# A two-layer transformer on one Trainium2 core: moved work in the pipeline of the first cross attention

## The reference

```python
q = rmsnorm((latent @ wq.T).reshape(B, S_q, H, D), q_norm_w)        # latent = layernorm(x)
k = rmsnorm((inputs @ wk.T).reshape(B, S_kv, HK, D), k_norm_w)      # inputs = ctx
v = (inputs @ wv.T).reshape(B, S_kv, HK, D)
attn = softmax(einsum('bkgqd,bksd->bkgqs', q, k))
x = x + einsum('bkgqs,bksd->bkgqd', attn, v).reshape(...) @ wo.T
```

## Time and profile before

| what | value |
|---|---|
| median of 3 runs | 1685.0 us (1678.43, 1685.0, 1685.45) |
| the profiled execution's own time | 1682.17 us |
| its span, first to last instruction | 1680.3 us |
| busy in the span | PE 1481.5, PEld 1233.8, DVE 1252.9, ACT 1119.4, POOL 894.1 us |
| mean granted TensorE clock | 0.967 of full speed |
| the first attention | from the start to about 465 us |

### The profile page before, as it was taken

One profiled execution on the slowest core, in us unless ns is written; L12 is line 12 of the kernel. 1 busy time (PEld: TensorE's weight loads), 2 busy tenths in 40 slices (PEclk: granted clock), 3 DMA queues, 4 the chain that ended last, 5 costly groups with the idle time before them and its releaser, 6 DMA issues.

```text
span 1680.3 us, 38581 instructions
## 1 busy us (share of the span) xinstructions
PE 1481.5 (88%) x12380; PEld 1233.8 (73%) x12443; DVE 1252.9 (75%) x3064; ACT 1119.4 (67%) x2631; POOL 894.1 (53%) x789
## 2 busy tenths in 40 slices
PE   4898888888877989898886899999889899999888
PEld 3777777677766876676765688888767688888766
DVE  6888888888856557777774788888655677777656
ACT  4887777677744547766674577787633687778632
POOL 4667777677631114444430777777500777777500
PEclk9999999999999999989997899999999899999999
DMA  9700000000012221100000000000000000000000
GB/s 384 296 1 10 11 10 10 7 17 12 12 59 67 85 84 43 33 13 16 16 14 4 10 16 16 15 14 15 10 12 3 6 15 15 16 15 14 10 18 38
DMA packets 75554, 61.30 MB, mean 36 GB/s; under 512 B 40256, under 2 KB 61120, under 8 KB 74688
## 3 DMA queue, kind: packets, MB, share of 16 engines
q1 hardware_dynamic: 71360, 51.69, 9.5%
q0 software_dynamic: 4096, 8.40, 1.7%
HBM read 21.30 MB, written 30.41 MB: 31 GB/s over the span
## 4 chain that ended last, share of the span: by engine, by line
PE 63%; DVE 17%; issue 7%; ACT 7%; POOL 3%; DMA 1%; SPq 0%; DVEq 0%; POOLq 0%; ACTq 0%
PE slot L459 6%; PE slot L1631 6%; PE slot L461 5%; PE slot L460 5%; PE slot L1614 4%; PE slot L1575 4%; PE slot L1584 3%; PE slot L1310 3%; PE slot L1649 3%; PE slot L516 3%; PE slot L1865 3%; PE slot L1361 2%; ACT c_pT L1386 2%; PE slot L1625 2%; PE slot L1176 2%
## 5 line engine op out<-in xcount | busy, mean ns | idle before, releaser
L1032 POOL TENSOR_TENSOR rs<-mv,nhalf 128x1 f32 (+1 forms) x160 | 98.6, 616 | 292.3 <-DVE mv L1027 222.7
L1781 POOL TENSOR_TENSOR d_A<-d_A,d_B 128x1024 f32<-128x1024 f32 x64 | 150.7, 2354 | 133.5 <-DVE d_B L1727 133.4
L1785 POOL TENSOR_TENSOR d_r<-d_vv,nhalf 128x16 f32<-128x16 f32 x64 | 186.5, 2914 | 47.8 <-DVE d_vv L1749 47.5
L731 ACT ACTIVATE d_p<-slot,d_nm,d_r 128x128 f32<-128x128 f32 x512 | 185.9, 469 | 25.8 <-DVE d_nm L1740 25.8
L731 ACT ACTIVATE a_p<-slot,a_nm,a_rq 128x77 f32<-128x77 f32 x512 | 164.0, 429 | 36.1 <-DVE a_nm L755 36.1
L1631 PE MATMUL slot<-d_v,d_pT 128*128 128x65 f32 x1024 | 121.8, 272 | 1.4 <-ACT d_pT L1668 1.4
L731 ACT ACTIVATE c_p<-slot,c_nm 128x77 f32<-128x77 f32 x512 | 117.5, 361 | 7.3 <-DVE c_nm L1416 7.2
L1631 PEld LDWEIGHTS slot<-d_v,d_pT 128*128 128x128 f32 x1024 | 119.4, 192 | 2.1 <-ACT d_pT L1668 1.8
L1708 DVE TENSOR_TENSOR d_A<-slot,T 128x1024 f32<-128x1024 f32 x64 | 78.3, 1224 | 49.8 <-PE slot L1575 49.6
L1386 ACT ACTIVATE c_pT<-slot 77x1024 f32<-77x1024 f32 x64 | 65.7, 1027 | 73.5 <-PE slot L1310 73.4
L1736 DVE TENSOR_REDUCE slot<-slot 128x8 f32<-128x1024 f32 x64 | 78.9, 1232 | 31.3 <-PE slot L1614 28.5
(11 more groups left out here) (285 smaller groups left out, 4607.2 us busy)
## 6 DMA issues: line engine op xcount, KB each, us to landing
routed<-zero SPq DMA_DIRECT2D x2, 9216.0 KB, 48.9
b_x<-routed SPq DMA_DIRECT2D x80, 64.0 KB
answers<-b_y SPq DMA_DIRECT2D x40, 128.0 KB
X<-in_x SPq DMA_DIRECT2D x2, 1024.0 KB, 7.4
d_zx<-Z SPq DMA_DIRECT2D x64, 32.0 KB
H<-Z SPq DMA_DIRECT2D x64, 32.0 KB
out<-f_o SPq DMA_DIRECT2D x8, 256.0 KB, 2.0
d_zx<-Z SPq DMA_DIRECT2D x64, 31.8 KB
```

Of the source, the lines that this page charges most:

```text
L731: i = e.activation(t["p"][:, h, :], R[slot][:, k // nbank, nk * (k % nbank):nk * (k % nbank) + nk], ACT.Exp, bias=t["nm"][:, h:h + 1], sca ...
L1032: return e.tensor_tensor(rs[:, bass.ds(b, 1)], mv[:, bass.ds(b, 1), 1:2].rearrange("p a b -> p (a b)"), nhalf[:, 0:1], ALU.pow)
L1781: e.tensor_tensor(t["A"][:, p, :], t["A"][:, p, :], t["B"][:, p, :], ALU.add).then_inc(S("d_key"), 1)
L1785: e.tensor_tensor(t["r"][:, it.m(2, 4), :], t["vv"][:, p, :], nhalf[:, 0:16], ALU.pow).then_inc(S("d_key"), 1)
```

## The change

Six things move in the loop of the first attention; the arithmetic stays the same.

- TensorE: the projection of k and v comes directly behind that of q, ahead of the transposes of P. The router's transpose comes behind both halves of the scores instead of between them, and its logits between the two halves of P times v.
- The square of k is taken by ScalarE out of PSUM (a new ACTIVATE) instead of by GpSimd, ahead of the copies of k and v.
- VectorE: the sums of k's squares and the router's layer norm come ahead of the copy of the transposed P; the second `largest` comes ahead of the router's choice; the sum of q's squares and a_vvq come behind `added`. The largest values are written into a free corner of the scores' own PSUM tile instead of into a_mx in SBUF.
- GpSimd: rk and kn come first in the step, then the context and the scatters; it divides both halves of P, takes the root for the layer norm behind them and rq last.
- Start: VectorE takes the first statistics ahead of the mask, and GpSimd writes its constant tables ahead of the first roots; later groups of roots come behind kn in the steps 1 to 3.
- Semaphore counts follow (a_ev has four events a step instead of three, a_k two instead of three).

```diff
-                b = it.b(3)
-                if b is not None:
-                    for half in range(2):
-                        turned(it, half)
-                b = it.b(1)
-                if b is not None:
                     if it.seen(2):
                         e.wait_ge(S("a_qTe"), it.upto(2))
                     e.wait_ge(S("ac_cl"), count(b))
                     passes(e, R[1][0:SK, 0, :], [c[:, it.m(1, 4), :] for c in a["c"]], [w[:] for w in wkv0])\
                         .then_inc(S("a_pj"), 1)
+                b = it.b(3)
+                if b is not None:
+                    for half in range(2):
+                        turned(it, half)
...
-                        if half == 1:
-                            router(it)
...
-                else:
-                    router(it)
-                logits(it)
-                values(it)
+                router(it)
+                values(it, lambda: logits(it))
...
+                b = it.b(1)
+                if b is not None:
+                    e.wait_ge(S("a_pj"), count(b, 2, 3))
+                    if past(b - 1):
+                        e.wait_ge(S("a_var"), count(b - 1, 1, 4))
+                    e.activation(a["sqk"][0:SK, :], R[1][0:SK, 0, 0:256], ACT.Square).then_inc(S("a_ev"), 1)
...
-                e.tensor_reduce(a["mx"][:, h], s, AX.X, ALU.max, negate=True).then_inc(S(("ac_mxa", "ac_mxb")[half]), 1)
+                mx = R[slot][:, 0, 4 * SK:4 * SK + 8]
+                e.tensor_reduce(mx, s, AX.X, ALU.max, negate=True).then_inc(S(("ac_mxa", "ac_mxb")[half]), 1)
 
                 e.wait_ge(S("a_rq"), count(b))
                 e.wait_ge(S(("ac_mxa", "ac_mxb")[half]), count(b))
-                e.tensor_tensor(a["nm"][:, h], a["mx"][:, h], a["rq"][:, it.m(2, 2), h], ALU.mult)\
+                e.tensor_tensor(a["nm"][:, h], mx, a["rq"][:, it.m(2, 2), h], ALU.mult)\
...
-                second_half(it)
-                row_normed(it)
-                b = it.b(2)
-                if b is not None:
-                    largest(b, it, 0, 2)
-                row_turned(it)
...
-                    e.wait_ge(S("a_k"), count(b, 1, 3))
+                    e.wait_ge(S("a_ev"), count(b, 2, 4))
...
-                    e.wait_ge(S("a_ev"), count(b, 1, 3))
-                    e.tensor_reduce(a["ssq"][:], a["sq"][:].rearrange("p (h d) -> p h d", d=DH0), AX.X, ALU.add)\
-                        .then_inc(S("a_var"), 1)
+                row_normed(it)
+                second_half(it)
+                b = it.b(2)
+                if b is not None:
+                    largest(b, it, 0, 2)
+                row_turned(it)
+                b = it.b(2)
+                if b is not None:
+                    largest(b, it, 1, 3)
                 row_chosen(it)
                 group_placed(it)
                 group_chosen(it)
-                b = it.b(2)
-                if b is not None:
-                    largest(b, it, 1, 3)
-                b = it.b(1)
-                if b is not None:
-                    e.wait_ge(S("a_var"), count(b, 3, 4))
-                    if past(b - 1):
-                        e.wait_ge(S("a_rq"), count(b - 1))
-                    e.tensor_scalar(a["vvq"][:], a["ssq"][:], 1.0 / DH0, RMS_EPS, ALU.mult, ALU.add)\
-                        .then_inc(S("a_var"), 1)
                 b = it.b(2)
                 if b is not None:
                     sums(b, 0)
...
                 added(it)
+                b = it.b(1)
+                if b is not None:
+                    e.wait_ge(S("a_ev"), count(b, 1, 4))
+                    e.tensor_reduce(a["ssq"][:], a["sq"][:].rearrange("p (h d) -> p h d", d=DH0), AX.X, ALU.add)\
+                        .then_inc(S("a_var"), 1)
+                b = it.b(1)
+                if b is not None:
+                    e.wait_ge(S("a_var"), count(b, 3, 4))
+                    if past(b - 1):
+                        e.wait_ge(S("a_rq"), count(b - 1))
+                    e.tensor_scalar(a["vvq"][:], a["ssq"][:], 1.0 / DH0, RMS_EPS, ALU.mult, ALU.add)\
+                        .then_inc(S("a_var"), 1)
                 b = it.b(2)
                 if b is not None:
                     sums(b, 1)
-                    e.wait_ge(S("a_sum"), count(b, 4, 4))
-                    normalize(e, a, slice(8, 16), SK).then_inc(S("ac_nb"), 1)
                 measured(it)
...
@@ -1055,42 +1058,42 @@
             def body(it):
                 if it.static and it.i == 7:
                     e.wait_ge(S("cleared0"), 16)
-                b = it.b(0)
-                if b is not None:
-                    split_context(e, a, it, b)
                 b = it.b(1)
-                if b is not None:
-                    e.wait_ge(S("a_ev"), count(b, 2, 3))
-                    if past(b - 1):
-                        e.wait_ge(S("a_var"), count(b - 1, 1, 4))
-                    e.tensor_tensor(a["sqk"][0:SK, :], a["kr"][0:SK, :], a["kr"][0:SK, :], ALU.mult).then_inc(S("a_k"), 1)
-                scatter(e, it)
                 if b is not None:
                     e.wait_ge(S("a_var"), count(b, 2, 4))
                     e.tensor_tensor(a["rk"][0:SK, :], a["vvk"][0:SK, :], nhalf[0:SK, 0:4], ALU.pow).then_inc(S("a_k"), 1)
-                    e.wait_ge(S("a_k"), count(b, 2, 3))
+                    e.wait_ge(S("a_ev"), count(b, 3, 4))
+                    e.wait_ge(S("a_k"), count(b, 1, 2))
                     if past(b - 1):
                         e.wait_ge(S("a_pj"), count(b - 1, 3, 3))
                     e.tensor_tensor(a["kn"][0:SK, :, :, :],
                                     a["kr"][0:SK, :].rearrange("p (h d) -> p h d", d=DH0).unsqueeze(2).to_broadcast([SK, 4, 2, DH0]),
                                     a["rk"][0:SK, :].unsqueeze(2).unsqueeze(3).to_broadcast([SK, 4, 2, DH0]),
                                     ALU.mult).then_inc(S("a_k"), 1)
+                if it.static and 1 <= it.i < NB // ST:
+                    first_roots(e, it.i)
+                b = it.b(0)
+                if b is not None:
+                    split_context(e, a, it, b)
+                scatter(e, it)
                 b = it.b(2)
                 if b is not None:
                     e.wait_ge(S("a_sum"), count(b, 2, 4))
                     normalize(e, a, slice(0, 8), SK).then_inc(S("ac_na"), 1)
+                b = it.b(2)
+                if b is not None:
+                    e.wait_ge(S("a_sum"), count(b, 4, 4))
+                    normalize(e, a, slice(8, 16), SK).then_inc(S("ac_nb"), 1)
+                b = it.b(4)
+                if b is not None:
+                    e.wait_ge(S("ac_ve"), count(b))
+                    root(e, b).then_inc(S("ac_rs"), 1)
                 b = it.b(1)
                 if b is not None:
                     e.wait_ge(S("a_var"), count(b, 4, 4))
                     if past(b - 2):
                         e.wait_ge(S("ac_expb"), count(b - 2))
                     e.tensor_tensor(a["rq"][:, it.m(1, 2), :], a["vvq"][:], nhalf[:, 0:16], ALU.pow).then_inc(S("a_rq"), 1)
-                b = it.b(4)
-                if b is not None:
-                    e.wait_ge(S("ac_ve"), count(b))
-                    root(e, b).then_inc(S("ac_rs"), 1)
-                if it.static and it.i < NB // ST - 1:
-                    first_roots(e, it.i + 1)
```

More of the change, by code:

```diff
@@ L409, in split_dve @@
             e.memset(r_["Ms"][:], 0.0).then_inc(S("r_Ms"), 4)
+            first_stats(e, 0)
             e.wait_ge(S("const_in"), 16 * N_CONST)
@@ L447, in start_pool @@
             e.tensor_scalar(order[:], order[:], 0.0, None, ALU.is_ge).then_inc(S("counted"), 1)
+            e.wait_ge(S("eps"), 3)
+            first_roots(e, 0)
         def rows(ap, b):
@@ L480, in router @@
                 if it.seen(1):
-                    e.wait_ge(S("a_ev"), nth(it.upto(1), 3, 3))
+                    e.wait_ge(S("a_ev"), nth(it.upto(1), 4, 4))
                 if it.static:
@@ L517, in turned, with values @@
                 mm.then_inc(S(("ac_PTa", "ac_PTb")[half]), 1)
-            def values(it):
+            def values(it, between=None):
                 b = it.b(3)
@@ L531, in values @@
                     for g in range(HK0):
+                        if g == 2 and between is not None:
+                            between()
                         for odd in range(2):
@@ L538, in values @@
                     mm.then_inc(S("ac_PV"), 1)
+                elif between is not None:
+                    between()
             def output(it, routed=True):
@@ L564, in body @@
                             e.wait_ge(S("ac_v"), it.upto(2))
-                    e.wait_ge(S("a_ev"), count(b, 3, 3))
+                    e.wait_ge(S("a_ev"), count(b, 4, 4))
                     for c in range(8):
@@ L576, in body @@
                         if it.seen(2):
[L577 removed]
+                            e.wait_ge(S("a_ev"), nth(it.upto(2), 4, 4))
                     if it.seen(1):
@@ L628, in body @@
```

(2 more changed lines are left out.)

10 lines of the change are left out of this document (2 added, 8 removed).

## The result

| | kernel before | changed kernel |
|---|---|---|
| median, same chip | 1682.0 us (10 runs) | 1668.9 us (10 runs, 1666.6 to 1675.2) |
| ratio, 95% interval | | 0.9923 [0.9905, 0.9941] |
| profiled execution, its span | 1682.2, 1680.3 us | 1670.9, 1668.7 us |
| busy PE, DVE, POOL in the span | 1481.5, 1252.9, 894.1 us | 1493.5, 1233.5, 912.9 us |
| first attention, steps 12 to 32 (copy of q at 163.67 or 161.81 to the last one) | 279.8 us | 271.0 us |

What follows compares the result with a forecast made beforehand. A loop through GpSimd's division, the root and a_rq was to bound the first attention at 12.94 us a step. Steps 12 to 32 gain 11.5 us, the start 1.8: 13.3 off 1682.2 gives 1669 us, range 1656 to 1686.

Steps and rivals of the forecast that it cites:

- the new loop: First attention, through GpSimd's division, the root and a_rq: 12.94 us a step, expected to bound the kernel.
- the hold of mv: mv, with two SBUF inputs, ends with GpSimd's division, so the root starts later: 0.25 us a step.
- rival E: A power on GpSimd holds VectorE too, delaying the router's layer norm: 15.0 us a step, 1722 us; 5%.
- Rival D: BN_STATS can't run beside GpSimd's division, root 0.8 us later: loop 13.7 us, 1690 us; 9%.
- The second loop: First attention, from GpSimd's division through TensorE's transposes to a_nm: 12.3 to 12.4 us, 0.5 shorter than the bounding loop.
- Rival B: mv isn't held by GpSimd's division: loop 12.69 us, 20.3 us gained, 1662 us; 21%.
- Group work: `chosen` and `places` in the first attention: their cost in four steps falls from 2.6 to 0.8 us.
- if plain steps stay at 13.0: Sign of a wrong forecast: steps without group work not becoming shorter; 12.9 us was expected.
- Eight steps: The eight steps before step 12 of the first attention: 103.9 us before and after, 0 gained.
- start: With GpSimd's tables first, TensorE's first transpose comes at 13.7 instead of 15.55 us: 1.8 us gained.
- one stop for tables of 5.3 us: Steps 12 to 32 of the first attention hold five fours of steps and this stop, counted with no change.
- Costed at nothing: Projecting k and v directly behind q costs TensorE no time, only giving sqk and the copies earlier.

Runs made afterwards that it cites:

- e1: Changed kernel with bn_aggr writing into mv and a one-column scalar addition instead of the instruction with two SBUF inputs: 0.993 of the kernel before.
- e2: Changed kernel with VectorE dividing the second half of P again instead of GpSimd: 0.9991 of the kernel before.
- r1: The changed kernel again, unaltered, against the kernel before on one chip in a later comparison: 0.996.
- e9: Changed kernel, TensorE waiting for h_gt only before q's projection, h_gt directly behind q's sum of squares, 14 other table instructions spread: 0.9893 of the kernel before.
- e3: Changed kernel with the sum of q's squares ahead of the router's choice instead of behind `added`: 0.9967 of the kernel before.
- e4: Changed kernel with the projection of k and v back behind the transposes of P: 1.0297 of the kernel before.

## Why the prediction was right, and where it was off

- **The bound and the new loop: right.** GpSimd closes the loop, through the root and a_rq. Counted from a_nm, the changed kernel has the first sum at 2.80 us (forecast 2.81), X 5.36 (5.35), the sum of squares 5.56 (5.64), the second sum 6.89 (6.95), GpSimd's division 8.00 (8.05), the root 9.41 (9.48), a_rq 9.97 (9.98), the next a_nm 12.90 (12.94). Nearly each term was one row of before, so only one had to be chosen between two values.
- **That one, the hold of mv: right in mechanism and size.** Forecast 0.25 us from the earlier trace rows; e1 took it out and the loop was 12.65. The rule of the Trainium skill cited in the prediction (SBUF — State Buffer, Who interferes with whom), that the loser is blocked to the end, agrees with mv, which ended with the division. Had the power a_rq held the router's layer norm as well (rival E), r_xn would have ended with it; r_xn took 0.35 us within a_rq, and rival E didn't come. Rival D didn't either: BN_STATS starts 0.15 us ahead of the division and takes 0.29 us, and the aggregation behind it takes 0.18 us within the division.
- **The second loop** was forecast 0.5 us shorter. VectorE idles 0.48 us ahead of a_nm, of which 0.11 is the hand-over that it always has behind a reduction: 0.4 shorter. Rival B's plain step came true in e1, but not B's time, since the steps with group work didn't follow: there VectorE waits for the router's transpose instead.
- **Group work, where most of the gain lies: right in mechanism, the cost taken 0.4 us too small.** 0.8 us in four steps forecast, 52.77 - 51.60 = 1.17 measured with the loop at 12.90 (0.41 for `chosen`, 0.77 for `places`); the sum of four came to 52.77 against 52.6.
- **The plain steps hardly moved.** The prediction took the old loop as 13.07 us, from one step; the nine plain steps average 13.00 by the copy of q, and 12.95 with the change (12.90 from a_nm to a_nm). So its sign of being wrong, "if plain steps stay at 13.0", is nearly met, although the loop is the one it described. A saving of 0.1 us a step couldn't have made the gain. What the new loop does is not to take the saving in group work back; in e2, with a loop 0.25 us longer, four steps are 53.67 us.
- **Eight steps, start:** 104.05 against 103.9 forecast; 2.0 against 1.8 us. The first transpose started at 12.84 us and not at 13.7; in the traces of r1 and e9, with the same start, it came at 12.40 and 13.68, so the agreement is in part luck.
- **The term that was wrong: "one stop for tables of 5.3 us" stayed unchanged in the sum.** The step grew by 2.1, from 18.37 to 20.45 us. 1.1 of it is h_gt coming later behind the addition to X, 1.0 is the way from h_gt to the next copy of q, with all nine projections at the lower clock. The larger part is the sum of q's squares behind `added`: with the sum at its earlier place the stop is 18.00 us (e3). The hold of mv is the smaller part ahead of h_gt, 0.4 us; without it the stop was 18.63 in e1, with a shorter stretch at the low clock, and 21.08 in e2, where VectorE divides. With the order of the queues in hand it could have been seen that h_gt stands behind that sum and behind mv. The steps 12 to 32 gained 8.8 us and not 11.5; 2.1 of the 2.7 missing are the stop, the rest the group work and the plain steps.
- **The sum.** Behind the last copy of q 0 was forecast and 0.95 us came. 8.8 - 0.15 + 2.0 + 0.95 = 11.6 us by the spans, 13.3 forecast. The medians differ by 13.1. So the loop and the group work were forecast rightly, the stop was missed by 2.1 us, and that the median came out at 1668.9 all the same is luck: the medians happen to differ by 1.5 us more than the spans. On another chip the same two kernels were only 0.4% apart (r1).
- **"Costed at nothing":** the move of k and v. e4 shows that the square of k on ScalarE, ahead of the copy of P in VectorE's queue, needs it: without it steps are 14.9 us and longer.

## What to carry to other kernels

When a cost is moved to an engine that idles, write down the closed loop that then runs through that engine, in starts from the trace, and add what each neighbour may be held for; here that gave the plain step within 0.1 us. Count separately the steps that carry extra work, for they can hold most of the gain: ask what covers that work before and after. Then walk all the places that aren't periodic (start, stops, end) with the same chain, since a wait that hides in the loop can be in the open there. And a bunch of small instructions at a stop is worth spreading: 4 us of table work in VectorE's gaps took 6 us from the stop (e9), against 11.6 between the spans for the whole change.

## What the hardware showed unexpectedly

- A product on GpSimd (kn, or the division of P, which is a product with the reciprocals of the sums) holds a VectorE TENSOR_TENSOR with both inputs in SBUF until its end (mv 0.72 against 0.16 us, a_nm up to 1.04 against 0.17), and also the TENSOR_SCALAR on 128x128 (0.71 against 0.34) and on 128x16 (a_vvq in the stop, 0.42 against 0.17), but not the one on 128x1 (0.15 us in all 32 cases), not BN_AGGR (0.18 us within the division), and not a_nm with one input in PSUM (at most 168 ns in 64 cases).
- GpSimd's power on 128x16 holds none of those that ran within it in this loop (r_xn 0.35 us inside a_rq, VectorE's division at most 804 ns).
- TensorE's clock fell to the lower level behind idle times of 4.03, 3.61, 2.94 and 2.86 us alike, but the low stretch lasted differently: with 2.86 us idle all nine projections ran at 0.63 us, with 3.61 only the first five did, and the nearly equal 2.94 us in the kernel before cost three slow ones and part of a fourth. Behind 2.59 us (e3) the transposes and two projections still ran at full speed, and the clock fell then, for the other seven.
- Chips differ: the changed kernel has a span of 1668.7 us on one and 1629.7 on another, and 37.6 of these 39 us lie behind the last copy of q.
